# Gated cross-attention and local-attention feed-forward, one core: layer norm by a centring product, feed-forward products in fp32, loops unrolled

## The reference

```
x = x + tanh(g_xattn) * xattn(layernorm(x), ctx_768, ...)
y = layernorm(x)
for l in range(2):
    h = shift_token(y);  q, k, v = split(h @ wqkv[l])
    q = l2norm(q) * q_scale;  k = l2norm(k) * k_scale;  q, k = rotary_xpos(q, k)
    y = y + local_attention(q, k, v) @ wo[l]            # 8 heads of 64, windows of 64
    h = shift_token(y)
    h = (h - mean(h)) / sqrt(var(h) + 1e-5) * lg + lb   # the feed-forward norm
    a, g = split(h @ w1 + b1)                           # 2 x 341 columns
    y = y + (a * gelu(g)) @ w2 + b2
x = x + tanh(g_ffn) * y
```

## Time and profile before

| | |
|---|---|
| time, three runs | 512.86, 514.04 (median), 515.69 us |
| span of the profiled execution, first to last instruction | 506.9 us |
| busy share of the span | DVE 83%, PE 76%, ACT 67%, POOL 57% |
| mean granted clock of PE | 0.954 of 2.4 GHz |
| the chain that ended last | DVE 51%, PE 24%, issue 15%, ACT 4%, POOL 3% |

### The profile page before, as it was taken

How to read it: one execution, slowest core, us unless ns; L and a number is a source line. 1 busy time by engine, 2 the same in 40 slices (tenths; PEclk the granted TensorE clock), 3 DMA queues, 4 the chain that set the end, 5 groups by cost and what they waited for, 6 DMA issues and landing times.

```text
span 506.9 us, 11211 instructions
## 1 busy us (share of the span) xinstructions
PE 386.1 (76%) x3636; PEld 306.5 (60%) x3636; DVE 419.8 (83%) x1329; ACT 338.7 (67%) x1075; POOL 286.7 (57%) x350
## 2 busy tenths in 40 slices
PE   0677777988878778776879578878778788768794
PEld 0466566766666566665657357666666566656572
DVE  2678677899999999998457668999999999984576
ACT  2456536787777777776466358777777777765565
POOL 5284036976667776765312278776667766763120
PEclk9978987999999999999989878999999999999899
DMA  7800000000000000000000000000000000000002
GB/s 183 269 0 1 1 1 2 1 3 1 0 0 0 0 0 0 0 1 3 1 0 0 0 1 3 0 3 1 0 0 0 0 0 0 2 1 1 0 0 83
DMA packets 10267, 7.14 MB, mean 14 GB/s; under 512 B 3245, under 2 KB 9447, under 8 KB 10238
## 3 DMA queue, kind: packets, MB, share of 16 engines
q1 hardware_dynamic: 8590, 5.63, 3.8%
q0 software_dynamic: 848, 1.15, 0.9%
q10 hardware_dynamic: 800, 0.00, 0.1%
HBM read 5.73 MB, written 1.05 MB: 13 GB/s over the span
## 4 chain that ended last, share of the span: by engine, by line
DVE 51%; PE 24%; issue 15%; ACT 4%; POOL 3%; DVEq 1%; DMA 1%; ACTq 0%; POOLq 0%
DVE shared L1086 11%; DVE ss L964 6%; DVE sm L1118 5%; DVE xs L1105 3%; DVE h_hi L957 2%; DVE sm L1123 2%; DVE hn_lo L1158 2%; PE ps L542 2%; DVE shared L971 2%; PE ps L543 2%; PE ps L544 2%; PE ps L576 2%; DVE h_lo L959 2%; DVE hnf L1133 1%; PE ps L663 1%
## 5 line engine op out<-in xcount | busy, mean ns | idle before, releaser
L387 POOL TENSOR_TENSOR shared<-shared,stab 128x256 f32<-128x256 f32 x128 | 105.4, 855 | 0.0
L370 POOL TENSOR_TENSOR shared<-shared 128x512 f32<-128x512 f32 x64 | 82.6, 1293 | 20.4 <-DVE shared L1086 17.0
L854 ACT ACTIVATE p<-sm,nm 128x128 f32<-128x128 f32 x128 | 49.8, 390 | 49.9 <-DVE nm L1118 49.9
L1086 DVE TENSOR_TENSOR shared<-shared,ctab 128x512 f32<-128x512 f32 x64 | 71.6, 1121 | 0.1
L375 POOL TENSOR_TENSOR p<-p,pri 128x512 f32<-128x512 f32 x32 | 33.2, 1039 | 60.9 <-DVE pri L1149 60.9
L429 PE MATMUL ps<-wqkv_hi,h_hi 128*128 128x512 f32 x96 | 46.5, 485 | 7.6 <-DVE shared L971 6.6
L964 DVE TENSOR_REDUCE ss<-sqr 128x16 f32<-128x1024 f32 x32 | 38.7, 1209 | 9.9 <-ACT sqr L729 9.8
L557 PE MATMUL ps<-idn,p 128*128 128x128 f32 x128 | 20.3, 281 | 32.5 <-POOL p L377 32.2
L971 DVE TENSOR_TENSOR shared<-ps,rr 128x1024 f32<-128x1024 f32 x32 | 38.8, 1214 | 5.5 <-ACT rr L738 5.5
L865 ACT ACTIVATE p<-sm,nm 128x64 f32<-128x64 f32 x128 | 42.6, 341 | 0.0
L729 ACT ACTIVATE sqr<-ps 128x512 f32<-128x512 f32 x64 | 35.5, 595 | 10.1 <-PE ps L431 9.4
(11 more groups left out here) (163 smaller groups left out, 1174.0 us busy)
## 6 DMA issues: line engine op xcount, KB each, us to landing
wqkv_raw<-in_L_ffn_wqkv_dram SPq DMA_DIRECT2D x1, 1536.0 KB, 13.2
out_dram<-shared SPq DMA_DIRECT2D x4, 256.0 KB, 2.5
w_raw<-in_L_ffn_w_dram SPq DMA_DIRECT2D x1, 682.0 KB
xt<-in_x_dram SPq DMA_DIRECT2D x2, 256.0 KB, 4.4
xt<-in_x_dram SPq DMA_DIRECT2D x1, 512.0 KB, 9.8
wo_raw<-in_L_ffn_wo_dram SPq DMA_DIRECT2D x1, 512.0 KB
ct<-in_ctx_dram POOLq DMA_DIRECT2D x1, 360.0 KB, 8.4
w_raw<-in_L_ffn_w_dram SPq DMA_DIRECT2D x2, 128.0 KB
```

Source lines behind the costliest of these rows:

```text
L370: T(qr[j][:, part], rc1[j][:, part], rs1[j][:, part], ALU.add).then_inc(rot_ready[j], 1)
L387: nc.gpsimd.tensor_tensor(s4[:, s, :, u, :], q4[:, s, :, 1 - u, :], tb, ALU.mult).then_inc(s_ready[j], 1)
L854: A(p1[j][:, c, :], sm1[j][:, c, :], ACT.Exp, bias=nm[j][:, c:c + 1], scale=-1.0, accum_out=psum_[j][:, c:c + 1]).then_inc(p_done[j], 1)
L1086: V.tensor_tensor(rc1[m.j][:, part].rearrange("p (h d) -> p h d", h=HEADS), qn[m.j][:, part].rearrange("p (h d) -> p h d", h=HEADS), ctab[ ...
```

## The change

- **Norm.** PE multiplies `xs` by `cen`, the identity less 1/128, so that the deviation from the mean stands in PSUM at once. ACT squares it there (a new instruction in its step, between the squares of q and k and the second four exponentials). DVE's one remaining instruction for the norm is `hn` = deviation in PSUM times `rstd`; it stands right behind the `xs` update at the start of the step. `dd`, `dsq` on DVE, `hnf`, `hn_hi` and `hn_lo` go. Since the deviation stays in its PSUM bank until the next step, the second scores product and the next centring product wait for `hn_ready`.
- **Feed-forward.** `hidden` and `back` are single fp32 products on `w1g`, `hn`, `w2_raw` and `uu`. The splits on ACT, DVE and POOL go, and the per-layer copies of weights too. `uu` has two buffers, and the output bank alternates between 6 and 7, so `update(g-1)` runs behind the gates of group g.
- **Loops.** All `Fori` loops become Python loops, so the program is straight code.
- DVE computes `cen` once, as its first work that waits for the identity's transfer.

```diff
+            V.tensor_tensor(cen[:], idn[:], ones[:], ALU.subtract).then_inc(cen_ok, 1)
 ...
-            with eng.Fori(0, (B - 6) // 2) as pair:
-                for n in (2, 3):
-                    step(lambda d, n=n: Batch(layer, pair, n + d), lambda d: True)
 ...
+                    if on(-2):
+                        pe.wait_ge(hn_ready[at(-2).j], at(-2).g + 1)
                     for c in range(PAIRS):
                         for a in (0, 64):
                             last = mm(ps[a:a + 64, S0, c * W:(c + 1) * W], qT[j][a:a + 64, c, 0:W], kT[j][a:a + 64, c, 0:W],
 ...
-                    mm(ps[:, S0, MEAN], ones[:], h_of(m.b), start=True, stop=True).then_inc(m_ps[j], 1)
+                    mm(ps[:, S0, DEV], cen[:], h_of(m.b), start=True, stop=True).then_inc(m_ps[j], 1)
 ...
-                    mm(ps[0:m, 2 * c + s, :], w1_hi[:, o2:o2 + m], hh, start=True, stop=False)
-                    mm(ps[0:m, 2 * c + s, :], w1_hi[:, o2:o2 + m], hl, start=False, stop=False)
-                    last = mm(ps[0:m, 2 * c + s, :], w1_lo[:, o2:o2 + m], hh, start=False, stop=True)
+                    last = mm(ps[0:m, 2 * c + s, :], w1g[:, layer, o2:o2 + m], hg, start=True, stop=True)
 ...
-                mm(ps[:, bank, :], w2_hi[0:m, c, :], u_hi[0:m, c, :], start=(c == 0), stop=False)
-                mm(ps[:, bank, :], w2_hi[0:m, c, :], u_lo[0:m, c, :], start=False, stop=False)
-                last = mm(ps[:, bank, :], w2_lo[0:m, c, :], u_hi[0:m, c, :], start=False, stop=(c == 2))
+                mm(ps[:, bank, :], w2_raw[0:m, layer, c, :], uu[gl_ % 2][0:m, c, :],
+                   start=(c == 0), stop=(c == 2)).then_inc(f_acc[c], 1)
 ...
+                if on(-1):
+                    m = at(-1)
+                    j = m.j
+                    act.wait_ge(m_ps[j], m.g + 1)
+                    A(dsq[j][:], ps[:, S0, DEV], ACT.Square).then_inc(d2_ready[j], 1)
 ...
-                V.tensor_copy(w1_hi[:], w1g[:]).then_inc(layer_w1, 1)
-                V.tensor_tensor(w1_lo[:], w1g[:], w1_hi[:].bitcast(F32), ALU.subtract).then_inc(layer_w1, 1)
 ...
+                if on(-2):
+                    m = at(-2)
+                    j = m.j
+                    dve.wait_ge(rstd_ready[j], m.g + 1)
+                    V.tensor_tensor(hn[:, bass.ds(m.b, 1), :].rearrange("p o n -> p (o n)"), ps[:, S0, DEV], rstd[j][:],
+                                    ALU.mult).then_inc(hn_ready[j], 1)
 ...
-                    V.tensor_tensor(hnf[j][:], dd[j][:], rstd[j][:], ALU.mult).then_inc(hnf_ready[j], 1)
-                    V.tensor_tensor(dd[j][:], h_of(m.b), ps[:, S0, MEAN], ALU.subtract).then_inc(d_ready[j], 1)
-                    V.tensor_tensor(dsq[j][:], dd[j][:], dd[j][:], ALU.mult).then_inc(d2_ready[j], 1)
-                    V.tensor_copy(hh, hnf[j][:]).then_inc(hh_ready[j], 1)
-                    V.tensor_tensor(hl, hnf[j][:], hh.bitcast(F32), ALU.subtract).then_inc(hn_ready[j], 1)
 ...
+                for g in range(NG):
+                    for c in range(3):
+                        gate(layer * NG + g, c)
+                    if g > 0:
+                        update(g - 1, layer * NG + g - 1)
```

More of the change, by code:

```diff
@@ L106, in build @@
         ones = sb("ones", [128, 128])
+        cen = sb("cen", [128, 128])
         epst = sb("epst", [128, 1])
@@ L139, in build @@
         xs = sb("xs", [D, B, N + 1])
-        hn_hi = sb("hn_hi", [D, B, N], F32R)
-        hn_lo = sb("hn_lo", [D, B, N], F32R)
+        hn = sb("hn", [D, B, N])
         bst = sb("bst", [128, GB, 6])
@@ L178, in build @@
         oT = sb2("oT", [128, PAIRS, N])
-        dd, dsq, lnl, rstd, hnf = (sb2(n, [D, N]) for n in ("dd", "dsq", "lnl", "rstd", "hnf"))
+        dsq, lnl, rstd = (sb2(n, [D, N]) for n in ("dsq", "lnl", "rstd"))
         cut = Carve()
-        gl, uu = cut(128, 3, 512), cut(128, 3, 512)
-        u_hi, u_lo = sb("u_hi", [128, 3, 512], F32R), sb("u_lo", [128, 3, 512], F32R)
+        gl = cut(128, 3, 512)
+        uu = [sb(f"uu{k}", [128, 3, 512]) for k in range(2)]
         stg = [cut(D, GB, N) for _ in range(2)]
@@ L234, in build, with __init__ @@
         class Batch:
[L237 removed]
+            def __init__(self, layer, n):
                 self.layer = layer
                 self.j = n % 2
[L240 to L241 removed]
+                self.g = layer * (B // 2) + n // 2
+                self.b = n
         def pipeline(eng, layer, step, first=-2, before={}):
[L248 to L251 removed]
+            for n in range(first, B + 2):
                 before.get(n, lambda: None)()
[L253 to L259 removed]
+                step(lambda d: Batch(layer, n + d), lambda d: 0 <= n + d < B)
         def groups(eng, first, both, last):
             first(0)
[L265 removed]
+            for g in range(NG - 2):
                 both(g, True)
@@ L654, in step @@
                 if on(0) and not on(1):
-                    hidden(0, 1, [1])
+                    hidden(at(0).layer, 0, 1, [1])
                 if on(0):
@@ L1209, in _ @@
-                gl_ = layer * NG + NG - 1
+                        V.scalar_tensor_tensor(out=t, in0=ps[q:q + 64, FB + gl_ % 2, :].rearrange("p (b n) -> p b n", b=GB),
+                                               scalar=lgb[q:q + 64, 2, gl_ // NG:gl_ // NG + 1], in1=t, op0=ALU.add, op1=ALU.add).then_inc(f_upd, 1)
+                dve.wait_ge(b1_done, 3)
+                for g in range(NG):
+                    for c in range(3):
+                        gate(layer * NG + g, c)
+                    if g > 0:
+                        update(g - 1, layer * NG + g - 1)
```

210 lines of the change are left out of this document (60 added, 150 removed).

## The result

| | before | changed |
|---|---|---|
| time, median | 513.45 us (four runs: 511.73 to 515.69) | 486.77 us (four runs: 486.15 to 488.90) |
| ratio | | 0.953, 95% interval 0.947 to 0.959 |
| span of the profiled execution | 506.9 us | 484.3 us |
| mask to mask, steps 2 to 11 | 10.85 us | 9.68 us |
| busy share | DVE 83%, PE 76%, ACT 67%, POOL 57% | DVE 69%, PE 81%, ACT 67%, POOL 57% |

The forecast was 506.4 us, range 499.5 to 512. The kernel came out 12.7 us under the range. In a second set of six runs it stood at 0.948 (0.943 to 0.953).

The account below looks back on a forecast made before the run. DVE was taken to bound the attention step, PE the feed-forward. Terms -11.0 + 0.4 - 0.8 - 5.8 + 8.6 - 2.0 + 2.6 + 0.4 = -7.6 us took 514.0 to 506.4 us, range 499.5 to 512.

Parts of the forecast that it names:

- the ring: Attention step: DVE's masks, ACT's exponentials, squares, `oT` and `rr`, then DVE's work to the next masks; sets the step's length.
- the feed-forward: PE's loop in each layer: 27 fp32 products cost 0.16 us more each, 4.3 us a layer, +8.6 in all, without gaps.
- steps 2 to 11, both layers: Attention loop: twenty steps fall from 10.85 to 10.3 us, 0.55 less each, -11.0 us.
- step 13: Attention step 13 falls from 10.97 to about 8.1 us, 2.9 less in each layer, -5.8 us.
- last steps: Steps 14 to 17: dearer products +0.8 and centring products waiting for `hn` +0.5, +1.3 a layer, +2.6 us.
- 9.54 + 0.27 + 0.28 + 0.2 = 10.3 us: Attention step after: step 0 without norm work, plus ACT's new square, DVE's `hn` and the wait for `rstd`.
- `hn`, 0.28, and the wait for `rstd`, 0.2: DVE, ahead of `h_hi` in each attention step: both lengthen the step, by 0.28 and about 0.15 to 0.2 us.
- ACT's square, 0.27: ACT's new 128x128 square ahead of the second exponentials lengthens each attention step by 0.27 us, bounds 0.25 and 0.6.
- Unrolling, nothing: Loops as straight code: a turn's branch costs at most 0.1 us, on an engine with slack, so no gain was counted.
- The prediction's own sign for a wrong bound: DVE's distance from mask to mask under 9.5 us would show that DVE's work was the bound.
- freed time counts in full: Rival, attention steps: waits for ACT shrink, steps fall to PE's 8.7 us, time near 474; chance 0.08 for all below 499.
- half of it: Half of the gain from DVE's freed time in the attention steps, 490 us; within the chance 0.08 for all below 499.

Follow-up runs that it names:

- both straight kernels with the old norm: Kernel before with its loops written out, 509.9 us; changed kernel with the norm of before put back, 499.95 us.
- the split one with the new: Kernel before as straight code with the new norm alone, feed-forward still split into `hn_hi` and `hn_lo`: 493.6 us, 0.962.
- `hn` twice: Changed kernel with the product `hn` done twice, once into a tile that nothing reads: 502.5 us, 0.984.
- `hn` behind the head: Changed kernel with `hn` placed behind `h_hi` and `h_lo` instead of ahead of them: 485.1 us, 0.947.
- the sine products left out: Kernel before with a memset of one column in place of each of POOL's four sine products of a step: 463.0 us, one run.
- The split kernel with the sine products held: Kernel before as straight code, old norm and splits, with POOL's sine products waiting until `h` is split: 493.6 us, 0.966.
- the run with the sine products held: Changed kernel with POOL's sine products waiting for `h_ready` of the next sequence: 483.55 us, 0.946.

## Why the prediction was wrong

The direction, the shape of the ring and the feed-forward were right; the size of the steps was not. By spans (506.9 to 484.3):

| part | forecast | measured |
|---|---|---|
| steps 2 to 11, both layers | -11.0 | -23.3 |
| step 1 | +0.4 | -0.8 |
| step 12 | -0.8 | -1.5 |
| step 13 | -5.8 | -4.9 |
| last steps and feed-forward, layer 0 | +5.3 | +6.0 |
| the same, layer 1 | +3.9 | +2.5 |
| start of layer 1 | 0 | -0.3 |
| start, to the masks of step 1 | +0.4 | -0.3 |
| sum | -7.6 | -22.6 |

(Forecast by layer: products 4.3, last steps 1.3, ends -0.3 and -1.7. Measured: from the masks of one step to those of the next in both traces.)

**The step that failed** is the sum "9.54 + 0.27 + 0.28 + 0.2 = 10.3 us". It was 9.68, and twenty such steps are 12.3 of the 15.0 us.
- *`hn`, 0.28, and the wait for `rstd`, 0.2*: both are there (0.21 and 0.18), and they cost nothing. From the update of `xs` to the masks it is 3.02 us before (129.67 to 132.69) and 3.00 after (126.65 to 129.65). `h_hi` gave 0.26 back, since it now starts where it need not wait for POOL. Most of the rest is 0.09 us between the start of the rotary product and the masks (1.24 us before, 1.15 after): ahead of the masks the marker no longer costs time of its own. That came with the new norm and not with the straight code, since it is 1.25 in both straight kernels with the old norm and 1.14 in the split one with the new; what frees it no run shows. I had taken 9.54 as DVE's own durations; what sets this stretch is when POOL's third sine product ends. `hn` twice, `hn` behind the head, the sine products left out and held, all four show it. The prediction had the sign of it in hand ("`hnf` (1.36 long, beside POOL)", in step 13) and didn't ask which other durations were of that kind.
- *ACT's square, 0.27*: on the ring, but 0.16. The row that I took it from, Ln at 0.25, was the nearest and too long (it also reads a bias tile, `epst`, which the square doesn't). 0.11 a step, 2.2 us.
- *What the sum comes to with both terms mended*: 9.54 + 0.16 = 9.70 us, against 9.68 measured.
- *Unrolling, nothing*: 0.09 a step, 2 us in all by its own run (10.85 to 10.76). The steps' miss holds none of it, since 9.54 was read from step 0, which is straight code in both kernels (9.54 and 9.56). The section of the Trainium skill that the prediction named there ties the stall to a taken branch whose target lies outside the code already fetched, a condition that the prediction left out.

**The view behind it.** "DVE bounds the step" rested on 10.49 busy of 10.81 us. The split kernel with the sine products held does the same work in steps of 10.17 (10.76 without the hold); with the sine products left out DVE's same instructions take 9.26. The prediction's own sign for a wrong bound, a step under 9.5, would not have shown this: 9.68 lies above it. The rival "freed time counts in full" (8.7 a step) didn't come true either: PE's 8.5 us of 9.68 and the waits of 0.56 and 0.73 show it; the truth lay between, at its "half of it" (490), by another mechanism.

**Step 13**: 8.56, not 8.1, in each layer. `w1_in` was off, 1.59 us beside POOL's sums and not 0.56, but the reciprocal behind it comes 3.80 us into the step (215.60 to 219.40), where I had 3.9. What is late are POOL's sums: they start 1.81 us into the step, where my 4.05 less 2.88 is 1.17, and take 3.11 and not 2.88, so that they end at 4.9 and not 4.05. `p` on POOL and PE's transposes ahead of the output product stand behind them, and the transposes of `p` start at 6.64 and not 6.15. The second sum, which runs beside `w1_in`, is probably held by it; no run tests that.

**The feed-forward** was right: 0.16 us a product, no gaps. In layer 1 it ended 1.4 us sooner than I had it, and that goes with the clock of the profiled execution: from the last masks to the end it took 52.50 us at a mean granted clock of 0.99, in the second profile of the same kernel 54.12 at 0.96, in before 50.02 at 0.95. At a like clock that is +4.1, against +3.9 forecast.

Behind this stands a rule of the Trainium skill, "SBUF — State Buffer", section Who interferes with whom: VectorE and GpSimd share a pair of SBUF ports under an exclusive lock; a VectorE instruction with two SBUF inputs, or a copy or cast in a two-port mode, contends with a GpSimd instruction that reads SBUF, the later one is blocked until the other is through, and one with at most one SBUF input outside those modes is not. The durations of this case agree: `hn` and `dd` (one PSUM input) last 0.27 to 0.29 us each of the 32 times in the kernels before and after, the reduction 1.21 to 1.22; `h_lo` goes from 0.29 to 0.71, `dsq` to 1.07, `hn_lo` to 1.14. The lock itself no profile shows, only what it would do. It was the rule to weigh ahead of the forecast.

## What to carry to other kernels

Ahead of adding up durations of a "full" VectorE, look for instructions of one form with two lengths, and set POOL's timeline beside them: where the longer ends fall on the ends of POOL's instructions, the time is a wait, and an instruction fed from PSUM can be had there for nothing, or 0.2 us more can cost 0.6. Such a wait is moved by holding the engine that is off the path for one semaphore, which gave 3% on the kernel before and, with `hn` behind the head, brought the changed one from 0.948 to 0.933. A time forecast goes from the median of the runs; whether the profiled execution was a quick one shows in its span against the others.

## What the runs showed of the hardware

- The blocking goes both ways. In the run with the sine products held, POOL's marker, 0.19 us alone, took 0.57 beside the rotary product, until that one ended; in before the fourth sine product, which meets the rotary product too, takes 1.19 us where the first takes 0.73.
- A 128x128 difference or product with both operands in SBUF takes 0.29 us alone, and 0.71 (`h_lo`), 1.07 (`dsq`) or 1.14 (`hn_lo`) beside POOL, by the length of the POOL instruction that it meets and by where in it it starts.
- ACT's square of 128x128 from PSUM costs its queue 0.16 us, Ln of the same shape 0.25.
- A true fp32 product of 512 columns takes as long as 3.7 fp32r ones (0.859 against 0.232), measured in the same place of the program.
- The half-clock stretch at the start of the feed-forward is not in every execution: the first profile of the changed kernel has it (granted clock 0.50 from 245.58 to 247.40, the loop's first four instructions take 2.48 us), the second doesn't (1.00 from 245.58 to 250.00, 1.96 us). PE idled 2.89 us just ahead of it in both.
